# A four-layer mixture-of-experts kernel: layers 1 to 3 from dense to sparse in blocks of 128 slots, the shared expert in front

## What is computed

```
layer 0: 48 kept experts (of 128), width 96,  top 8, at most 96 tokens each
layer 1:  8 experts, width 176, top 2, silu(c Wg)*(c Wu) Wd, and a shared expert of width 352
layer 2: 14 experts, width 176, top 2, the same form,        and a shared expert of width 352
layer 3: 16 experts, width 128, top 2, relu(c Wup)^2 Wdown, weights packed as integers with scales
y[token] = sum over the chosen experts of gate * expert(c[token])  (+ shared(c[token]))
```

## Time and profile before

| | |
|---|---|
| median of 3 runs | 772.42 us (772.38 to 773.41) |
| the profiled execution | 773.22 us, of which the span in the trace is 771.4 us |
| PE busy | 639.2 us, 83% |
| DVE busy | 581.6 us, 75% |
| POOL busy | 389.6 us, 51% |
| ACT busy | 262.8 us, 34% |
| moved by DMA | 49.19 MB |

### The profile page before, as it was taken

The page is one execution under the profiler, slowest core; times in us unless marked ns, Lnnn a source line. Parts: engine busy times, 40 slices in busy tenths (PEclk is TensorE's granted clock), DMA queues, the critical chain, the costliest instruction groups (busy, mean ns, idle before and its releaser), DMA issues.

```text
span 771.4 us, 9946 instructions
## 1 busy us (share of the span) xinstructions
PE 639.2 (83%) x3123; PEld 468.5 (61%) x3123; DVE 581.6 (75%) x947; ACT 262.8 (34%) x504; POOL 389.6 (51%) x299
## 2 busy tenths in 40 slices
PE   0030315999999889999998899999999996999997
PEld 0020314777778667777766577777777765666665
DVE  6999693999999746777756477777773367688785
ACT  1310042222222633333327333333333344444452
POOL 4733585999995325555523245555553223334433
PEclk9999999999999889999999899999999998799999
DMA  9000002555551102111111021111111111122211
GB/s 282 25 28 0 1 28 67 149 162 158 154 146 30 35 8 52 49 53 49 45 41 42 10 63 48 48 48 48 48 48 54 31 56 57 48 71 78 84 56 54
DMA packets 49281, 49.19 MB, mean 64 GB/s; under 512 B 4192, under 2 KB 40160, under 8 KB 49248
## 3 DMA queue, kind: packets, MB, share of 16 engines
q1 hardware_dynamic: 47520, 44.06, 19.4%
q0 software_dynamic: 1728, 4.72, 2.0%
HBM read 46.67 MB, written 2.10 MB: 63 GB/s over the span
## 4 chain that ended last, share of the span: by engine, by line
PE 72%; DVE 17%; POOL 4%; issue 3%; ACT 2%; DMA 1%; DVEq 0%; SPq 0%; POOLq 0%; ACTq 0%
PE y_ps L443 20%; PE g_ps L388 19%; PE u_ps L388 12%; PE y_ps L578 8%; PE u_ps L551 4%; PE g_ps L432 4%; POOL R L1386 3%; DVE fwd L895 2%; PE g_ps L566 2%; PE u_ps L432 2%; DVE fwd L884 2%; DVE bwd L885 2%; DVE w_lo L1213 1%; DVE A L1096 1%; PE r_ps L536 1%
## 5 line engine op out<-in xcount | busy, mean ns | idle before, releaser
L1333 POOL TENSOR_TENSOR h_lo<-h,h_hi 128x512 fp32r<-128x512 f32 x104 | 139.0, 1336 | 281.0 <-ACT h_hi L857 281.0
L857 ACT ACTIVATE h_hi<-h 128x512 fp32r<-128x512 f32 x104 | 65.7, 632 | 180.9 <-DVE h L1294 180.2
L1014 DVE TENSOR_TENSOR t<-act_g,u_ps 128x512 f32<-128x512 f32 x72 | 48.5, 673 | 94.9 <-PE u_ps L388 92.3
L443 PE MATMUL y_ps<-h_hi,w_hi 128*128 128x512 f32 x208 | 93.4, 449 | 0.5 <-ACT h_hi L857 0.5
L388 PE MATMUL g_ps<-c_hi,w_hi 128*128 128x512 f32 x208 | 87.6, 421 | 3.8 <-POOL c_lo L1333 1.3
L388 PE MATMUL g_ps<-c_lo,w_hi 128*128 128x512 f32 x208 | 84.9, 408 | 0.0
L388 PE MATMUL g_ps<-c_hi,w_lo 128*128 128x512 f32 x208 | 84.7, 407 | 0.0
L811 ACT ACTIVATE act_g<-g_ps 128x512 f32<-128x512 f32 x104 | 61.7, 593 | 66.0 <-PE g_ps L388 65.5
L443 PE MATMUL y_ps<-h_hi,w_lo 128*128 128x512 f32 x208 | 82.4, 396 | 0.0
L1347 POOL TENSOR_TENSOR fwd<-fwd,bwd 128x512 f32<-128x512 f32 x32 | 44.1, 1378 | 47.7 <-DVE bwd L885 47.6
L443 PE MATMUL y_ps<-h_lo,w_hi 128*128 128x512 f32 x208 | 66.0, 398 | 0.9 <-POOL h_lo L1333 0.9
(11 more groups left out here) (188 smaller groups left out, 1280.9 us busy)
## 6 DMA issues: line engine op xcount, KB each, us to landing
raw<-in_wglu SPq DMA_DIRECT2D x36, 320.0 KB, 2.9
wup<-in_wglu SPq DMA_DIRECT2D x36, 256.0 KB, 3.7
wdn<-in_wglu SPq DMA_DIRECT2D x12, 384.0 KB, 4.2
raw<-in_wglu SPq DMA_DIRECT2D x36, 128.0 KB, 2.1
raw_q<-in_wq SPq DMA_DIRECT2D x16, 256.0 KB
raw_s<-in_s_up SPq DMA_DIRECT2D x32, 64.0 KB
raw_s<-in_s_down SPq DMA_DIRECT2D x16, 128.0 KB
fs<-in_fT SPq DMA_DIRECT2D x2, 512.0 KB, 4.9
```

The lines of the kernel that those rows point to most:

```text
L443: return pe.matmul(y_ps[:, m, hf, :], w[:, slot, DN0 + m * P:DN0 + (m + 1) * P], r[:, k % HB, :], start=start and first, stop=False, skip_ ...
L857: act.activation(h_hi[:, k % HB, :], h[:, k % 2, :], ACT.Copy).then_inc(h_hi_ready, 1)
L1014: dve.tensor_tensor(t[:, par, :], act_g[:, par, :], other, ALU.mult).then_inc(t_ready, 1)
L1333: return pool.tensor_tensor(dst, src, hi.bitcast(F32), ALU.subtract)
```

## The change

**Layers 1 to 3.** The router now chooses two experts for each token (`choose`, `gates_of`), counts positions within each expert with products of zeros and ones (`positions2`), and gives each of the 2048 (token, choice) pairs a slot (`slots`). The slots of an expert begin at a multiple of 128. A block is 128 slots, all of one expert; there are always 16 + experts − 1 of them, so `BK` = 23, 29 and 31, together 83; some are part empty or empty. `lists2` and `read_lists2` make the token of each slot, `block_experts` the expert of each block (`be`).

For a block, POOL gathers 128 rows of `ctab` (128 KB), PE transposes them (2 instructions), ACT moves them to SBUF, PE multiplies up in plain f32 (in layers 1 and 2 eight products of 128 columns; each f32 product stands as two in the trace), ACT and DVE make the hidden values, PE multiplies down (2 products of 256 columns), ACT copies the result out and POOL scatters it to `ybuf` in HBM. In layer 3 it is 2 products up and 1 down. SP reads the number of the block's expert into a register and loads its weights: 360 KB up and 180 KB down in layers 1 and 2, twice 128 KB in layer 3. There are three buffers for weights, four for gathered rows, three for results.

After the last block of a layer SP loads `ybuf` back (twice 1 MB), and PE puts the two rows of each token together with its two gates (`final`: 32 f32 products of 128 columns for each half, with `diag`, a diagonal matrix of gates).

**The shared expert** of layers 1 and 2 is no longer part of the chunks. It runs dense, in plain f32, in six pieces of 128 (or 96) columns by 512 tokens, all in front of the layer's blocks. The router's steps lie between the pieces.

**Weights.** The up weights of layers 1 and 2 lie in HBM in chunks of 128 columns. ACT copies them into a table `wx` in which an expert's 176 columns lie together: eight transfers within HBM, of 14 x 128 x 128 or 22 x 128 x 128 numbers, in pieces of 512 bytes (18,432 pieces, 9.4 MB). The packed weights of layer 3 are unpacked in layers 1 and 2: in two of every four blocks SP loads a packed expert (`load_q`) and stores the previous one to `w3`, DVE and ACT unpack it.

**Layer 0's front.** The sums of WKV move from POOL to PE (`wkv_sums`: four f32 products of 256 columns and two of 512, a unit). The small constants are loaded ahead of the second half of f and x.

**Unchanged**: layer 0's groups, and WKV for later layers behind groups and blocks.

```diff
--- before.py
+++ after.py
-CH = [CH0, -(-(E1 * I1 + SH1) // P), (E2 * I2 + SH2) // P, E3]
+NE = [0, E1, E2, E3]
+BK = [0] + [2 * TT + n - 1 for n in NE[1:]]
+NSH, SHEAD = 6, 6
+XB, OB, WB = 4, 3, 3
...
+            def load_block(layer, b):
+                n = B0[layer] + b
+                w = n % WB
+                wait(sp, bd_done, n - WB + 1)
+                e = sp.value_load(be[0:1, b:b + 1], min_val=0, max_val=NE[layer] - 1)
+                if layer < 3:
+                    sp.dma_start(wU[:, w, :, :], wx[layer][:, :, bass.ds(e * I1, I1)]).then_inc(w_in[w], 16)
+                    sp.dma_start(wD[:, w, :, :], flat[bass.ds(e * I1 + row0(layer), I1), DN0:DN0 + C]
+                                 .rearrange("(h i) n -> i h n", h=2)).then_inc(w_in[w], 16)
...
+                for b in range(WB, BK[layer]):
+                    e = unpacked(layer, b - WB)
+                    if e is not None:
+                        store_w3(e)
+                        if e + 2 < E3:
+                            load_q(e + 2)
+                    load_block(layer, b)
...
+            pe.wait_ge(minus_ready, 1)
+            wkv_sums(0)
+            wkv_sums(1)
             renumber_gate()
+            wkv_sums(2)
+            wkv_sums(3)
             logits0(0)
...
+                if shared:
+                    shared_up(layer, 0)
+                    shared_up(layer, 1)
+                    shared_down(layer, 0)
+                positions2(layer)
+                if shared:
+                    shared_up(layer, 2)
+                    shared_down(layer, 1)
+                lists2(layer)
+                if shared:
+                    for k in range(3, SHEAD):
+                        shared_up(layer, k)
+                        shared_down(layer, k - 1)
+                    shared_down(layer, SHEAD - 1)
+                block_turn(layer, 0)
+                for b in range(BK[layer]):
+                    if b + 1 < BK[layer]:
+                        block_turn(layer, b + 1)
+                    block_up(layer, b)
+                    if b:
+                        block_down(layer, b - 1)
+                block_down(layer, BK[layer] - 1)
+                for hf in range(2):
+                    final(layer, hf)
...
             for hf in range(2):
                 sigmoid_x(0, hf)
+            for layer in (1, 2):
+                for q in range(2 * KT):
+                    act.dma_start(wx[layer][:, q, :].rearrange("p (c n) -> p c n", n=P),
+                                  wglu[sum(CH[:layer]):sum(CH[:layer + 1]), :, q * P:(q + 1) * P]
+                                  .rearrange("c p n -> p c n")).then_inc(wx_in, 16)
             act.wait_ge(gwt_done, 1)
             act.activation(gwn[:, :], r_ps[:, 0:C], ACT.Copy).then_inc(gwn_ready, 1)
...
+                for b in range(BK[layer]):
+                    block_hidden(layer, b)
+                    if layer < 3 and b < 4 * QN[layer]:
+                        wkv_part(Q0[layer] + b // 4, b % 4)
+                    e = unpacked(layer, b)
+                    if e is not None:
+                        unpack(e)
```

More of the change, by code:

```diff
@@ L36 @@
 XG = 6
[L37 to L44, removed]
+NE = [0, E1, E2, E3]
+BK = [0] + [2 * TT + n - 1 for n in NE[1:]]
+B0 = [sum(BK[:l]) for l in range(NL)]
+IH = I1 // 2
 KG = [0, 2 * (E1 + 1), 2 * (E2 + 1), 2 * E3]
@@ L65, in wait, with unpacked @@
         eng.wait_ge(sem, value)
[L68 to L98, removed]
+def unpacked(layer, b):
+    e = 2 * (b // 4) + b % 4 + 2 * QN[1] * (layer - 1)
+    return e if layer < 3 and b % 4 < 2 and b < 4 * QN[layer] and e < E3 else None
 def build(nc, xT, fT, cond, wu, o2n_row, o2n_col, gwT, rconst, gscale, wglu, wq, s_up, s_down, sel3,
@@ L493, in logits0, with turn_c @@
                 mm.then_inc(logits0_done, 1)
[L495 to L497 removed]
+            def turn_c(layer, hf):
+                wait(pe, ctok_ready, 4 * layer + 2 * hf)
                 for n in range(TH // 2):
@@ L657, in _ @@
-                steps(pe, layer, body, more=4)
+                shared = layer < 3
+                for hf in range(2):
+                    logits(layer, hf)
+                    turn_c(layer, hf)
+                if shared:
[7 more added lines that the diff above has]
+                lists2(layer)
@@ new lines, in _ @@
+                shared = layer < 3
+                sigmoid_x(layer, 0)
+                sigmoid_x(layer, 1)
+                store_c(layer, 0)
+                if layer == 2:
+                    scores_silu(layer)
+                    store_c(layer, 1)
+                    router_exp(layer)
+                else:
+                    router_exp(layer)
+                    store_c(layer, 1)
+                if shared:
+                    for k in range(SHEAD):
+                        shared_silu(layer, k)
@@ L1000, in add_y @@
                 else:
-                    last = max(k for k in range(2 * CH[layer]) if place(layer, k)[1] == hf)
-                    dve.wait_ge(y_done, S0[layer] + last + 1)
+                    dve.wait_ge(fin_done, 2 * (layer - 1) + hf + 1)
                 for m in range(KT):
@@ L1322, in _ @@
-                steps(dve, layer, body, wkv)
-                if layer < NL - 1:
-                    first_up_lo(layer + 1)
-                add_y(layer, 1)
-                if layer < NL - 1:
-                    cond(layer + 1, 1)
+                if shared:
+                    shared_product(layer, 0)
+                    shared_product(layer, 1)
+                slots(layer)
+                block_experts(layer)
+                read_lists2(layer)
+                if shared:
+                    for k in range(2, SHEAD):
+                        shared_product(layer, k)
```

972 lines of the change are left out of this document (526 added, 446 removed).

## The result

The changed kernel takes 836.27 us (median of 4 runs, 825.38 to 838.52) against 772.75 us, a ratio of 1.082; two of its runs lie over 1.5% above its fastest, and without them (825.38 and 834.49 are left, middle 829.9) it is 1.074, 95% interval 1.064 to 1.084. Forecast were 829 us and a range of 750 to 890.

What follows compares the result with a forecast made beforehand. PE's work bounded the dense layers; the weights' landing was to bound the blocks. Front +38, ahead 43 + 46 + 27, blocks 341, behind 22.3 + 22.3 + 23.5, on 264 with 1.8 outside the span: 829 us, range 750 to 890.

Steps and rivals of the forecast that it cites:

- What comes last in a block: Blocks of layers 1 and 2: the weights' landing decides; two periods are one load plus 1.9 + 0.9 us of PE.
- The way L: A block's weight load in layers 1 and 2: wake-up, register load, arithmetic, first issue and landing, 5.7 us together.
- The period of a plain block: Layers 1 and 2, block without packed expert: (5.7 + 2.8)/2 = 4.3 us, 3.8 to 4.8 with the register load's ends.
- rival 3: Blocks of layers 1 and 2: waits keep PE's clock at 0.5, 6.2 us a block, 909 us in all; chance 0.08.
- The packed experts: Layers 1 and 2: their loads on SP raise a block's period to 5.8 us, the mean with two in four to 5.05.
- The front: Ahead of layer 1: ACT held by its table transfers, plus WKV sums and small table operations, +38 us; +12 if not held.
- The hold: Front: ACT held while issuing 9.4 MB of table transfers, until 62 us (between 50 and 85); DVE loses 33 us.
- the sums on PE: Front: WKV sums on PE (7 us cold) with ten small table operations cost some 5 us more.
- Rival 1: Front: ACT isn't held by its table transfers, eight issues take 4 us; front +12, 803 us in all; chance 0.20.
- Ahead of the blocks: Shared expert and router work before the blocks: 43 us in layer 1, 46 in layer 2, 27 in layer 3.
- Behind the blocks: Result scattered, `ybuf` loaded back, final products: 22.3 us each in layers 1 and 2, 23.5 in layer 3, nothing hidden.
- Rival 2: Blocks: weights' landing hidden, PE sets 3.4 to 3.6 us, POOL 2.9 in layer 3; 734 us, 760 with held front; chance 0.22.

Runs made afterwards that it cites:

- e6: Changed kernel with four useless f32 products on PE ahead of the weights' wait in every second block of layers 1 and 2; 828.98 us.
- e3: Changed kernel without unpacking layer 3's experts (loads, DVE and ACT work, stores); layer 3 reads other rows of the same size; 824.38 us.
- e1: Changed kernel with the eight table copies issued by SP behind the first two groups' loads instead of by ACT; 820.88 us.
- e5: Changed kernel with table copies on SP, five buffers for weights, six for gathered rows, four for results; 718.00 us, 0.928 of the dense kernel.
- e8: Changed kernel with five buffers for weights, six for gathered rows, four for results, table copies left on ACT; 744.00 us.
- e4: Changed kernel with only one of two channel blocks used in the up part of layers 1 and 2, loads and waits kept; 830.67 us.

## Why the prediction was right, and where it was not

The direction and the cause that was named for it, the weights' way with ACT's hold beside it, came true; that the time came within 7 us of 829 is luck, since the stages were wrong by 8 to 30 us each and their errors nearly cancel.

**What comes last in a block** was named rightly: the weights' way through three buffers, two periods for one way and two parts of PE's work. The way L was forecast at 5.7 us and is 6.6 for the block at 645.05 and 5.9 for the one at 634.22, whose buffer came free at 628.30. Its parts were off in opposite directions. For the block at 645.05, wake-up, register load and arithmetic took 0.94 us from 638.47 to 639.41 where 1.3 were put; the register load in it, put at 1.0 us, is 0.43 in the median. The first issue, put at 0.5, took 1.08 until the second began at 640.49 (0.76 for the block at 634.22), and the landing, taken at 3.9 us, is 4.6 from 640.49 to 645.05. The trace of the changed kernel, the load of the expert's number, then POOL's scatters, durations min/median/max in ns:

```profile
L350 SPq TENSOR_LOAD <-be x83: 262/432/1091, 307.4 to 806.5; - x83
...
L1524 POOL DMA_INDIRECT ybuf<-o_s,idx_s x83: 969/1002/1901, 332.8 to 814.8; - x83
```

The Trainium skill, "DMA: Bandwidth & Descriptors", section "Latency and other measured facts", has a floor of about 0.6 us for it. Here the median is 0.43 and the shortest 0.26, so the measurement decides against that floor.

**The period of a plain block** was forecast at 4.3 us and is 5.2. The failed step is PE's 1.9 + 0.9 us in it: in the loop, the up part that comes after the wait runs at half the clock, 3.4 us. I had this as rival 3, and dismissed it for the forecast with the argument that PE at 6.2 us would have no wait and hence the full clock. The true state lies between, a wait and a slow part in every second block, and I said "a mixture at most" without giving the mixture a price. (6.6 + 3.4 + 0.9)/2 = 5.4 would have been the sum, with a way of 5.9 us 5.1; measured are 5.23. In e6, with the clock at 1.00, the period is 4.48, near the 4.3.

**The packed experts**, put at +0.75 on 32 blocks, 15 us in layer 1 and 9 in layer 2, cost 13.7 and 8.8 by e3, so this term was right. Layer 3 (3.2) came to 2.9, and POOL's scatter, priced like the gather at 0.95, is 1.00.

**The front** was +38 and is +18.3. That ACT is held was right and its consequence, DVE's idle time behind PE, too. Too large were two terms. The hold was put at 34 us, until 62; it is 24.3, until 48.7. ACT began to issue at 22.24 already, beside the sigmoids, and the 9.4 MB moved at 308 GB/s (24 to 54 us, share 1.06), where 288 and a chance of half of that had been put. Some of it, until about 54.5 us, moved when ACT was free again. And the sums on PE, put at 5 us of loss, with the rest of the front's changes are a gain of 4.6: the third sum took 5.2 us, the fourth 3.6, DVE stood 6 us further on than before when its wait began (its scans end at 30.86, before at 36.93), and it may have got something from POOL's relief (below). Rival 1, that ACT isn't held, is refuted: the eight transfers of 0.9 to 1.4 MB held ACT for 26.4 us and, in e1, SP for 28.5. The rule of the Trainium skill, "DMA: Bandwidth & Descriptors", section "Issuing engines are not separate DMA queues", that issuing is usually small beside the transfer, does not hold for them.

**Ahead of the blocks** 116 against 125: the bare router chain of layer 3 is 30.8, not 27, and the pieces of the shared expert hide less of it. **Behind the blocks** 68 against 60: in layer 1 PE starts on `ybuf` 8.8 us behind the last down part, as forecast (8.9). Its two halves together take 9.9 us and not 10.6 (they are 16 products of 128 columns each, 32 rows of the trace, and not 32 products), and the first half's addition, sigmoid and product with R, put at 2.8 us behind the second half, lie beside it.

**Rival 2**, faster at 734 with the weights hidden, was not this kernel; it is nearly e5 (718), whose blocks take 277 us, 3.34 each, under the 3.7 from which the sparse form was to win. (Layer 2's 99 us in this rival's sum should be 101.) The 462 us put outside the blocks are 441 in e5, so that 4.0 a block would have been even there.

## What to carry to other kernels

Where loads go through n buffers and the part that frees a buffer lags one block behind, the period is at least (way of the load + the work that holds the buffer) divided by n − 1. This fits the measured periods for three buffers (5.1 to 5.4 against 5.23); with four and five something else came last, so the division is not tried there. Count the way from the freeing of the buffer to the landing before settling on n: here the buffers alone stand between a gain of 3.5% (e8) and a loss of 7%. Give large or many transfers to an engine that has nothing to do for as long as they take to move, since here the issuer was held at the pace of the data. And price a regular wait on PE with the slow work behind it.

## What the runs showed of the hardware that I had not expected

- Behind waits of 2.7 to 3.5 us PE's up part took 3.3 to 3.7 us in place of 1.91, every second block (granted clock 0.53 from 634.3 to 637.3). In e5 the up part behind a wait of 1.58 us (at 547.63) took 1.91, and one behind 1.85 us (at 344.14) took 3.71. A quarter of PE's instructions taken away in e4 changed its busy time from 38.5 to 39.2 us in 55.
- Transfers within HBM in pieces of 512 bytes moved at 308 GB/s (changed kernel, 24 to 54 us, share 1.06); the loads of the kernel before into SBUF moved at 332.
- Reading one number into a register of SP took 0.43 us in the median, 0.26 at the least.
- The comparison of 128 x 1536 elements on DVE takes 1.75 to 2.59 us, 2.12 in the mean of four, in the kernel before from 103.53 on, beside six operations of POOL of 24.9 us together. Each takes 1.75 in e1, where POOL stands idle. The same operation, the same size; that POOL is the cause is argued and was not tried.
